# Channel attention: two slots' scores interleaved over four row groups, then one block of products

## The reference, cut to what matters

```python
q = einsum('oc,bct->bot', Wq, target) + bq     # target = layernorm(x) * mask
k = einsum('oc,bcs->bos', Wk, source) + bk     # source = ctx * mask
v = einsum('oc,bcs->bos', Wv, source) + bv
# 16 heads of 8 channels
dot = einsum('bhdt,bhds->bhts', q, k) / sqrt(8)
dot = mask * dot - (1.0 - mask) * 1e6
amap = softmax(dot, axis=-1) * mask
out = einsum('bhts,bhds->bhdt', amap, v)
x = x + tanh(g) * out
```

## Time and profile before

| | us |
|---|---|
| median of three runs | 1780.16 |
| lowest and highest run | 1776.92, 1786.28 |
| the profiled execution | 1787.89 |
| its span | 1786.1 |
| steady batches of channel attention, busy in 16 us: PE, DVE, ACT | 15.58, 14.76, 13.36 |

### The profile page before, as it was taken

The page is one execution under the profiler, slowest core; times in us unless marked ns, Lnnn a source line. Parts: engine busy times, 40 slices in busy tenths (PEclk is TensorE's granted clock), DMA queues, the critical chain, the costliest instruction groups (busy, mean ns, idle before and its releaser), DMA issues. The chain is left out here.

```text
span 1786.1 us, 34417 instructions
## 1 busy us (share of the span) xinstructions
PE 1701.8 (95%) x11824; PEld 1431.4 (80%) x11832; DVE 1162.9 (65%) x2556; ACT 996.9 (56%) x2526; POOL 566.4 (32%) x624
## 2 busy tenths in 40 slices
PE   8999997699899999999999999999999998899997
PEld 6666664357788899898898988988988997689985
DVE  5799997898556656656657655555555567854434
ACT  2588885586555545545556545445455553555543
POOL 3233323553521111111113111111111212877773
PEclk9899998799999999999999999999999999999999
DMA  6011122112100100100100021001000004443347
GB/s 205 14 32 37 34 85 96 27 49 99 51 13 1 48 13 13 37 13 13 36 20 30 13 64 34 15 1 37 13 1 13 1 1 117 147 118 116 128 126 270
DMA packets 48825, 97.45 MB, mean 55 GB/s; under 512 B 7370, under 2 KB 29050, under 8 KB 47668
## 3 DMA queue, kind: packets, MB, share of 16 engines
q1 hardware_dynamic: 40071, 72.57, 13.2%
q0 software_dynamic: 7584, 21.37, 4.0%
q10 hardware_dynamic: 1000, 1.26, 0.2%
HBM read 73.85 MB, written 20.97 MB: 53 GB/s over the span
## 5 line engine op out<-in xcount | busy, mean ns | idle before, releaser
L2288 POOL TENSOR_TENSOR hold_wq<-hold_wq,ca_rsum 128x512 f32<-128x512 f32 x128 | 134.1, 1047 | 797.9 <-DVE ca_rsum L2530 797.9
L2148 ACT ACTIVATE hold_wq<-ca_pT 128x512 f32<-128x512 f32 x128 | 76.4, 597 | 381.2 <-PE ca_pT L2355 381.2
L1054 DVE TENSOR_REDUCE a_mx<-a_s 128x2 f32<-128x512 f32 x256 | 167.2, 681 | 37.0 <-PE a_s L904 35.6
L797 ACT ACTIVATE a_prob<-a_s 128x512 f32<-128x512 f32 x256 | 147.7, 602 | 68.7 <-PE a_s L924 68.3
L2511 DVE COPY ca_values<-ca_v 128x512 f32<-128x512 f32 x128 | 88.3, 690 | 124.8 <-PE ca_v L2307 124.2
L2305 PE MATMUL ca_qk<-early_x,cw_wqkv_h 128*128 128x512 f32 x384 | 160.9, 419 | 1.3 <-PEq L1507 1.3
L2520 DVE TENSOR_TENSOR hold_wq<-ca_s,hold_wk 128x512 f32<-128x512 f32 x128 | 88.2, 689 | 108.1 <-PE ca_s L2348 108.0
L2307 PE MATMUL ca_qk<-early_x,cw_wqkv_l 128*128 128x512 f32 x384 | 151.6, 395 | 0.0
L2306 PE MATMUL ca_qk<-early_x,cw_wqkv_h 128*128 128x512 f32 x384 | 151.1, 393 | 0.0
L2428 PE MATMUL ca_acc<-ca_wo_h,ca_oT_l 128*128 128x256 f32 x512 | 145.0, 283 | 0.0
L2427 PE MATMUL ca_acc<-ca_wo_l,ca_oT_h 128*128 128x256 f32 x512 | 144.8, 283 | 0.0
(11 more groups left out here) (537 smaller groups left out, 4756.2 us busy)
## 6 DMA issues: line engine op xcount, KB each, us to landing
early_big<-slot_results SPq DMA_DIRECT2D x16, 512.0 KB, 9.0
mw_raw<-in_d_expert_w SPq DMA_DIRECT2D x12, 352.0 KB, 5.3
a_wraw<-a_heads SPq DMA_DIRECT2D x32, 128.0 KB, 2.1
a_heads<-a_osb SPq DMA_DIRECT2D x124, 32.0 KB
mw_down<-in_d_expert_d SPq DMA_DIRECT2D x1, 2816.0 KB
token_rows<-early_rows SPq DMA_DIRECT2D x1, 2176.0 KB, 14.9
hold_wk<-in_c_wkT SPq DMA_DIRECT2D x1, 2064.0 KB
hold_wq<-in_c_wqT SPq DMA_DIRECT2D x1, 2064.0 KB
```

Of the source, the lines that this page charges most:

```text
L797: act.activation(prob[:, w % PR, :, :], s2_bank(w)[:, :, :], ACT.Exp, scale=1.0 / A_ROOT)\
L1054: dve.tensor_reduce(mx[:, b % 2, :, h], s1_bank(b, u)[:, :, :], AX.X, ALU.max)\
L2288: pool.tensor_tensor(prob[:, k % 2, :, :], prob[:, k % 2, :, :], rsum[:, k % 2, :].unsqueeze(2).broadcast_to([P, GB, TOKENS]), ALU.mult)\
```

## The change

The slots are taken in pairs (t even, t + 1), `DOUBLES`.

- PE makes the scores of both slots first, half by half: c=0 of the first scores of t and t + 1, c=0 of the second scores of t and t + 1, then the same for c=1. In this order neighbouring matmuls lie in four different row groups. Then come the biases of both slots, and then the other products of t and of t + 1 (`products`). In `products` the turned maxima come last of the batch's work, and they move from u = 2 to u = 1, so that their use of the `s1` ring is the third of a batch, not the fourth (`TURN_USE` = 2). The two halves of `project_v` are split over u = 13 and u = 15.
- ACT does for each pair: what stands ahead of the exponentials for both slots (reading maxima, rounding a piece, now at u = 2, 6, 10, 14, reading values at u = 0, copying outputs at u = 4 and 12, scaling the mask, normalising x), then both exponentials, then the rest.
- DVE takes the maxima of both slots of a pair at its even slot, then the rest in the old order.
- SP moves the maxima of a batch in one transfer of 16 rows instead of four.

The same instructions are issued in all, except for three transfers per batch that fall away.

```diff
@@ turned / copied
-            return b if t % U == 2 and 0 <= b < BATCHES else None
+            return b if t % U == 1 and 0 <= b < BATCHES else None
-            b, rest = divmod(t - A_LAG - (12 if t > ALL + 6 else 11), U)
+            b, rest = divmod(t - A_LAG - 12, U)
+        DOUBLES = range(SLOTS.start, SLOTS.stop, 2)
+        TURN_USE = 2
         def s1_use(b, u):
-            return (U + 1) * b + u + (1 if u >= 3 else 0)
+            return (U + 1) * b + u + (1 if u >= TURN_USE else 0)
@@ s1_free
-            if i == 3:
+            if i == TURN_USE:
                 after(eng, mT_ready, b)
             else:
-                eng.wait_ge(max_ready, min(U * b + (i if i < 3 else i - 1) + 1, ALL))
+                eng.wait_ge(max_ready, min(U * b + (i if i < TURN_USE else i - 1) + 1, ALL))
@@ sync: maxima
-                    for r in range(A_SLOTS):
-                        row = A_ROWS * r + 27
-                        sp.dma_start(qs[row:row + 1, b % A_BUFS, :, :].bitcast(F32),
-                                     mT[A_TILES * r:A_TILES * r + A_TILES, b % 2, :].bitcast(F32))\
-                            .then_inc(m_in[b % 2], 16)
+                    sp.dma_start(qs[27:P:A_ROWS, b % A_BUFS, :, :].bitcast(F32), mT[:, b % 2, :].bitcast(F32))\
+                      .then_inc(m_in[b % 2], 16)
@@ scalar
-                for t in SLOTS:
-                    if unit2(t):
-                        exponential(t - A_LAG)
+                def before_exponentials(t):
                     u = t % U
-                    if turned(t) is not None:
-                        read_maxima(turned(t))
-                    if built(t) is not None and u in (1, 5, 9, 13):
-                        round_piece(built(t), *PIECES[u - 1])
-                    if built(t) is not None and u == 14:
-                        read_v(built(t))
+                    if turned(t - 1) is not None:
+                        read_maxima(turned(t - 1))
+                    if built(t) is not None and u in (2, 6, 10, 14):
+                        round_piece(built(t), *PIECES[u - 2])
+                    if u == 0 and 0 <= t < ALL:
+                        read_v(t // U)
+                    if copied(t) is not None:
+                        copy_out(*copied(t))
+                        if copied(t)[1] == 0:
+                            gated_mask(copied(t)[0])
                     if prepared(t) is not None and u == 0:
                         normal_x(prepared(t))
...
+                for first_t in DOUBLES:
+                    for t in (first_t, first_t + 1):
+                        before_exponentials(t)
+                    for t in (first_t, first_t + 1):
+                        if unit2(t):
+                            exponential(t - A_LAG)
+                    for t in (first_t, first_t + 1):
+                        behind_exponentials(t)
@@ tensor
-                for t in SLOTS:
-                    one, two = unit1(t), unit2(t)
-                    for c in range(2):
-                        if one:
-                            first(*one, c)
-                        if two:
-                            second(*two, c)
+                def products(t):
                     u, b = t % U, built(t)
-                    if b is not None and b >= WHOLE_ROWS and u in PIECES:
-                        bias(b, *PIECES[u])
-                    if turned(t) is not None:
-                        turn_maxima(turned(t))
                     if weighed(t):
                         weigh(*weighed(t))
                     if b is not None:
                         if u in (0, 4, 8, 12):
                             project(b, *PIECES[u], 0)
                             project(b, *PIECES[u], 1)
-                        if u == 13:
-                            project_v(b)
+                        if u in (13, 15):
+                            project_v(b, (u - 13) // 2)
+                    if turned(t) is not None:
+                        turn_maxima(turned(t))
...
+                for first_t in DOUBLES:
+                    both = (first_t, first_t + 1)
+                    for c in range(2):
+                        for t in both:
+                            if unit1(t):
+                                first(*unit1(t), c)
+                        for t in both:
+                            if unit2(t):
+                                second(*unit2(t), c)
+                    for t in both:
+                        if built(t) is not None and built(t) >= WHOLE_ROWS and t % U in PIECES:
+                            bias(built(t), *PIECES[t % U])
+                    for t in both:
+                        products(t)
@@ vector
                 for t in SLOTS:
-                    if unit1(t):
-                        take_max(*unit1(t))
+                    for n in ((t, t + 1) if t in DOUBLES else ()):
+                        if unit1(n):
+                            take_max(*unit1(n))
```

More of the change, by code:

```diff
@@ L780, in read_maxima @@
                     if b >= 2:
-                        act.wait_ge(m_in[b % 2], 64 * (b // 2))
-                    use = (U + 1) * (b + 1) + 3
+                        act.wait_ge(m_in[b % 2], 16 * (b // 2))
+                    use = (U + 1) * (b + 1) + TURN_USE
                     act.activation(mT[:, b % 2, :], s1[use % S1_BANKS][0:A_HEADS, 0, :], ACT.Copy, scale=-1.0)\
@@ L806, in copy_out, with behind_exponentials @@
                         .then_inc(out_copied, 1)
-                for t in SLOTS:
-                    if unit2(t):
-                        exponential(t - A_LAG)
+                def before_exponentials(t):
                     u = t % U
-                    if turned(t) is not None:
-                        read_maxima(turned(t))
-                    if built(t) is not None and u in (1, 5, 9, 13):
-                        round_piece(built(t), *PIECES[u - 1])
-                    if built(t) is not None and u == 14:
-                        read_v(built(t))
+                    if turned(t - 1) is not None:
[8 more added lines that the diff above has]
+                            gated_mask(copied(t)[0])
                     if prepared(t) is not None and u == 0:
                         normal_x(prepared(t))
[L820 to L823, removed]
+                def behind_exponentials(t):
                     if gram_made(t) is not None:
@@ L876, in project, with project_v @@
                         mm.then_inc(psum_s, 1)
-                def project_v(b):
-                    if b < WHOLE_ROWS:
+                def project_v(b, t):
+                    if b < WHOLE_ROWS and t == 0:
                         freed(pe, b, "v", 0)
                     w = slice(1024, 1152)
-                    for t in range(2):
-                        c = slice(P * t, P * t + P)
-                        o = proj[bank_of(b, "v", 0)][:, t, 0:P]
-                        if b < WHOLE_ROWS:
-                            pe.matmul(o, mext[:, DIM * b + P * t:DIM * b + P * t + P], bext[:, w], start=True, stop=False)
-                        pe.matmul(o, ch[:, b % 2, c], wh[:, w], start=False, stop=False, skip_group_check=b >= WHOLE_ROWS)
-                        pe.matmul(o, ch[:, b % 2, c], wl[:, w], start=False, stop=False, skip_group_check=b >= WHOLE_ROWS)
-                        mm = pe.matmul(o, cl[:, b % 2, c], wh[:, w], start=False, stop=True, skip_group_check=b >= WHOLE_ROWS)
-                    mm.then_inc(v_psum, 1)
+                    c = slice(P * t, P * t + P)
+                    o = proj[bank_of(b, "v", 0)][:, t, 0:P]
+                    if b < WHOLE_ROWS:
+                        pe.matmul(o, mext[:, DIM * b + P * t:DIM * b + P * t + P], bext[:, w], start=True, stop=False)
+                    pe.matmul(o, ch[:, b % 2, c], wh[:, w], start=False, stop=False, skip_group_check=b >= WHOLE_ROWS)
+                    pe.matmul(o, ch[:, b % 2, c], wl[:, w], start=False, stop=False, skip_group_check=b >= WHOLE_ROWS)
+                    mm = pe.matmul(o, cl[:, b % 2, c], wh[:, w], start=False, stop=True, skip_group_check=b >= WHOLE_ROWS)
+                    if t == 1:
+                        mm.then_inc(v_psum, 1)
                 def first(b, u, t):
@@ L914, in second @@
                         if v == 0:
-                            pe.wait_ge(m_in[b % 2], 64 * (b // 2 + 1))
+                            pe.wait_ge(m_in[b % 2], 16 * (b // 2 + 1))
                         if w < len(s2):
```

## The result

The changed kernel takes 1799.74 us in the median of four runs (1788.81 to 1806.87), beside 1779.12 us for the kernel before in four runs on the same chip. The ratio is 1.0097, with a 95% interval of 1.0065 to 1.0130: slower by 1% (the two medians alone give 1.0116). The forecast was 1789.8, in a range from 1768 to 1804.

A forecast was written before the change was run, and what follows sets the result against it. Three engines hand work round in a ring, DVE nearly full, none alone setting the time. Steady batches +15.8, head -2.3, slots 24 to 54 -1, last batch -3.6, tail +0.7 make +9.6: 1780.2 becomes 1789.8 us, range 1768 to 1804.

The forecast's parts named there:

- The chain of a steady batch: Steady batches, followed step by step from the start of pair (6,7): period 16.95 us against 15.59, +1.36 a batch.
- The term of the sum: Steady batches, slots 54 to 240: the longer period over 11.6 batches adds 15.8 us.
- One bound: Steady batches: if both bias waits were nothing, the same chain would give a period of 15.7 us.
- The bias waits: PE's values' and query biases wait for DVE's key splits: about 0.4 to 0.6 us, twice a batch.
- Rival (a): Steady batches: no bias waits, or PE does not hold what is queued behind; period 15.7, total 1775 us; chance 0.22.
- Head, last batch, slots 24 to 54: Time saved outside the steady batches: head -2.3 us, slots 24 to 54 -1, last batch -3.6.
- Tail: End of the part: the third weight sum stands behind four more scores, +0.7 us (bounds 0, 1.5).
- Rival (b): Steady batches: DVE becomes the one bound with no idle left, period 14.1 us, total 1757; chance 0.11.
- Rival (c): Steady batches: PE's clock may fall to half near pair (12,13); two falls more, +12.8 us, total 1803; chance 0.17.

The follow-up runs named there:

- the second profile of the changed kernel: The changed kernel run again without any edit on another chip, beside the kernel before: median 1799.49 us over six runs, ratio 1.0087.
- the filled wait: Changed kernel with the bias of slot 12 of a batch issued three times instead of once, ahead of the values' bias: 1786.11 us, ratio 1.0009.

## Why the prediction was right or wrong

**The chain of a steady batch: right in the order of its steps, 0.4 us too long.** Its zero is the moment at which pair (6,7) gets its last bank; in the profile of after that is 200.37. Then, predicted and measured: split of the first key piece 6.44 and 6.28; projection behind the waiting bias 7.60 and 7.44; pair (14,15) 8.86 and 8.63; pair (0,1) 10.79 and 10.56; query bias 11.41 and 11.16; turned maxima 12.73 and 12.41; pair (2,3) 13.05 and 12.72; pair (4,5) 15.09 and 14.69; the next (6,7) 16.95 and 16.52. Three terms were too big: DVE's leg to the split by 0.16; a projection that is followed by full-height matmuls takes 0.82, not the 0.90 that I took from one followed by scores, twice; and ACT's legs in (2,3) and (4,5) by 0.1 together. The term of the sum was +15.8 and is 11 to 12. One bound does not follow from its steps: without the two bias waits (0.76 and 0.35) the same chain gives 15.84, not 15.7.

**The bias waits: right for the first, half of it for the second.** Rival (a) falls: PE holds back what stands behind a waiting bias. The longer of the two is 0.52 us a batch, where I had said 0.4 to 0.6 for each; the second, at the query bias, is 0.3 at most. The prediction gave it 0.35, but its own prices of scores and bias (0.45 and 0.42) put the projection at 11.66 without a wait, against 11.83 with it: 0.17. The list has 9.8 us of them in all, where I had named 8 to 12. I had not asked whose order is to blame, though: taking the maxima singly is worth 1.0 us a batch, moving the bias 0.4.

**Head, last batch, slots 24 to 54: right in sign and nearly in size.** The fall at 59 us vanished from the first profile, which I had not foreseen; it was to the good of that execution, and the second profile of the changed kernel has a short one there (58.4 to 61.9). Tail: wrong by 0.7, the third weight sum is waited for 0.61 us in both kernels. And the prediction says that the clock fell once in this part; before, it also fell behind 300 us, in the tail (it changes no term of the sum).

**Rival (b), DVE as the one bound: falls.** DVE idles 34.0 us instead of 15.7. Only in the plain order with single maxima does it come near, with a period of 15.29 against the 14.1 of its own need. The Trainium skill ("TensorEngine Tiling (Array Packing)", PSUM Bottleneck) has it that tiling speeds up TensorE but not the reading of PSUM. The traces agree so far that no order of PE's scores here came below 15.29; that the reading sets this limit they do not show, since DVE still waits 17.4 us for scores there.

**Rival (c), the clock: came true, beside the forecast and not in its place.** This is where the sum went wrong: it put the clock at nothing in the steady batches. I gave the falls a case of their own (0.17) with two falls of 6.4, on the pattern of the earlier trace rows. Measured, they came in every second batch of the profiled run, each 3.5 us long and 1.0 dear, and most other runs had a lower clock still: 0.0095 of mean clock between the medians, about 11 us. The chain and the clock are not alternatives. The wait of 0.5 us that the chain contains is also what goes before the falls, so a case with the wait and without falls was not the likeliest one. With the chain's true 4.0 and 11 for the clock the sum is +15, and the kernel on its second chip is 14.7 slower than before. On the first it is 20.6; what is over there is within the spread of four runs.

**How much was luck.** The forecast of 1789.8 said slower, and slower it was, inside the range. But head, steady batches and last batch alone come to +4.0 us, which the prediction itself would have called no change (half a per cent is 8.9). The steady batches were put 4 us too dear and the clock 11 us too cheap, and the first error covered part of the second. That the change came out clearly slower is the work of the clock, for which the sum had nothing; the range was wide enough to hold either outcome.

The Trainium skill ("TensorE: Matmul & The Clock Gate", Part 1) ties half speed in its table to an idle, cold engine, and tells further on of a kernel whose TensorE idles for very short times between groups of matmuls and swings between the two speeds. The traces here are nearer to the second than to the first: in front of the falls PE was still 0.49 to 1.00 busy in each microsecond, and its longest standstill there was 0.5 us.

## What to carry to other kernels

When work is taken in pairs, look at the engine that hands results back in the middle of a pair: its small outputs (here the key splits) move behind the second member, and since PE's matmuls here never passed a waiting one, one maximum of delay became standstill on two engines. Pair the engine that gains by it (PE, ACT) and leave the other one in single steps: that version is 0.8 to 0.9% faster than before, and with plain order of the scores 0.8 to 1.0%. If the time of a kernel scatters, put its runs beside their mean clock before you explain the median by one profile, and when an edit moves the times, look in the profiles whether the falls went with them: with the filled wait they had not gone.

## What was not expected of the hardware

- Time and mean granted clock of an execution lie on a line for these kernels, to within some 2 us: 11.8 us per 0.01 for the changed kernel (10 runs), 12.0 for the kernel before (62 runs).
- Stretches at 1.2 GHz came in steady work in which no standstill of TensorE was longer than 0.5 us. In the two profiles of the changed kernel they began 0.5 to 0.7 us behind such a wait in the one and 1.5 us behind it in the other: six short ones in one profiled run, one of 10 us in the other. Most batches had the wait and no fall; what draws one is open.
- With four superfluous matmuls in that wait (all six take 0.87 us, two take 0.39) the median of the kernel is 13 us lower (ratio to before 1.0009 for 1.0087), though its profile has more half clock in the steady batches and not less.
